# Scatters of a counting sort that wait one by one, four more blocks of it moved that way, and a reciprocal shared by two divisors

## The reference, cut to what matters

```python
# mixer of layer 0: linear attention on (1, 3125, ...) after a 5-tap convolution
q = relu(q); k = relu(k)
vk  = einsum('ngdl,ngel->ngde', v, k)
out = einsum('ngde,ngdl->ngdl', vk, q)
out = out / (sum(v, -1, keepdims=True) + 1e-15)     # with one position: v / (v + 1e-15), per element

# graph part of layer 0's feed-forward: 65536 random edges
e     = leaky_relu(a_src[src] + a_dst[dst])
alpha = exp(e - segment_max(e, dst)[dst]);  denom = segment_sum(alpha, dst)
agg   = segment_sum(h[src] * alpha / denom[dst], dst)
```

## Time and profile before

| | |
|---|---|
| time, median of 3 runs | 3484.07 us |
| profiled execution: span from first to last instruction | 3089.4 us |
| what lies around the span (median minus span) | 394.7 us |
| PE busy | 2176.1 us, 70% |
| DVE busy | 1707.6 us, 55% |
| POOL busy | 1668.6 us, 54% |
| ACT busy | 1346.5 us, 44% |
| mean granted PE clock | 0.844 |

### The profile page before, as it was taken

The page is one execution under the profiler, slowest core; times in us unless marked ns, Lnnn a source line. Parts: engine busy times, 40 slices in busy tenths (PEclk is TensorE's granted clock), DMA queues, the critical chain, the costliest instruction groups (busy, mean ns, idle before and its releaser), DMA issues. The chain is left out here.

```text
span 3089.4 us, 46006 instructions
## 1 busy us (share of the span) xinstructions
PE 2176.1 (70%) x14802; PEld 1673.9 (54%) x14802; DVE 1707.6 (55%) x3862; ACT 1346.5 (44%) x3168; POOL 1668.6 (54%) x1597
## 2 busy tenths in 40 slices
PE   4487292563399998376601586887786399999998
PEld 4362152453366665364301375666665266999997
DVE  7889545898311222989876666766665840111113
ACT  3368334774221221257903417677763021334432
POOL 0246564566277777877732555777772226344441
PEclk9799696787599999599955797888877589999999
DMA  3130034200223223245133345666662123356335
GB/s 91 62 123 1 18 67 78 49 1 1 42 49 83 43 43 76 48 117 118 10 94 60 62 122 187 214 212 203 201 206 89 51 80 92 120 195 222 122 123 130
DMA packets 183715, 301.48 MB, mean 98 GB/s; under 512 B 90826, under 2 KB 142653, under 8 KB 173096
## 3 DMA queue, kind: packets, MB, share of 16 engines
q1 hardware_dynamic: 104412, 168.04, 18.5%
q0 software_dynamic: 79168, 131.91, 16.1%
HBM read 266.22 MB, written 105.72 MB: 120 GB/s over the span
## 5 line engine op out<-in xcount | busy, mean ns | idle before, releaser
L1899 POOL DMA_INDIRECT ge_near<-gat_src,s_other x512 | 527.1, 1030 | 163.3 <-issue 157.2
L3253 POOL DMA_INDIRECT he_buf<-wh_dram,s_other x400 | 389.2, 973 | 160.4 <-issue 121.2
L982 POOL DMA_INDIRECT pl_table<-s_key,s_other x272 | 310.4, 1141 | 256.5 <-DMA pl_table<-s_key,s_other 181.9
L2764 ACT ACTIVATE x_hT<-bank,x_w 128x128 f32<-128x128 f32 x448 | 164.4, 367 | 262.6 <-PE bank L2707 231.4
L3373 ACT ACTIVATE he_buf<-he_buf,he_e 128x128 f32<-128x128 f32 x800 | 236.4, 386 | 2.8 <-issue 0.4
L2266 DVE TENSOR_TENSOR XN<-bank,arena 125x256 f32<-125x256 f32 (+1 forms) x100 | 42.5, 425 | 307.8 <-PE bank L2234 307.8
L2707 PEld LDWEIGHTS bank<-x_xT,x_w 128*128 128x128 f32 x1792 | 208.7, 192 | 2.8
L2707 PE MATMUL bank<-x_xT,x_w 128*128 128x128 f32 x1792 | 209.0, 275 | 0.0
L2717 PE MATMUL bank<-x_w,x_hT 128*128 128x256 f32 x896 | 202.5, 380 | 0.0
L3485 DVE SCALAR_TENSOR_TENSOR he_buf<-he_buf,he_cont 128x256 f32<-128x256 f32 x375 | 182.9, 488 | 29.2 <-issue 0.9
L2234 PE MATMUL bank<-arena 128*125 128x256 f32 x800 | 181.7, 385 | 23.2 <-ACT arena L2247 23.2
(11 more groups left out here) (749 smaller groups left out, 5694.1 us busy)
## 6 DMA issues: line engine op xcount, KB each, us to landing
he_result<-he_buf SPq DMA_DIRECT2D x25, 2080.0 KB, 7.8
XN<-s_a_dram SPq DMA_DIRECT2D x57, 512.0 KB
x_y<-XN SPq DMA_DIRECT2D x24, 448.0 KB
ge_near<-gat_src,s_other POOLq DMA_INDIRECT x512
x_x<-zero SPq DMA_DIRECT2D x1, 7196.0 KB, 44.2
x_xs<-x_x SPq DMA_DIRECT2D x56, 128.5 KB, 2.1
he_buf<-wh_dram,s_other POOLq DMA_INDIRECT x400
arena<-x_y SPq DMA_DIRECT2D x2, 2800.0 KB
```

The source lines that it names most:

```text
L982: pool.indirect_dma_start(out=self.table, out_offset=bass.IndirectOffsetOnAxis(ap=self.goal[:, c:c + 1], axis=0), in_=self.val[:, c:c + 1] ...
L1899: pool.indirect_dma_start(out=G[:, c, 0:HF + H], out_offset=None, in_=m.gat_src, in_offset=bass.IndirectOffsetOnAxis(ap=ed.other[:, c:c + ...
L2764: act.activation(self.hT[u % 2][:, f, :], m.ps[f % 4][:, 0:TS], ACT.Gelu, bias=self.rb1[u % self.B][:, f:f + 1]).then_inc(self.racted, 1)
L3253: pool.indirect_dma_start(out=buf[j][:, c, 0:HF + H], out_offset=None, in_=m.wh_dram, in_offset=bass.IndirectOffsetOnAxis(ap=ed.other[:, t ...
```

## The change

- `send`: three semaphores take turns. Scatter c waits, before it is issued, for scatter c-3 alone. The wait behind each third one is gone, also that behind the last of a stage.
- `BLOCKS` is 21 instead of 17: 336 scatters instead of 272, and 11 instead of 15 blocks in the product moves. They are dealt out as 64 in four batches with a `learn` each and 62 behind the fifth (126 in the sort), 34 at the start of `mix0_start` and 14 behind its gathers, 162 in `mix0_attention`.
- `load` waits for the three semaphores.
- `attend`: the 2048 divisors of a group (per partition) are cut into halves a and b. With va' = va + 1e-15 and vb' = vb + 1e-15 it forms va'·vb', takes one reciprocal of 1024 elements, and multiplies va by vb' and vb by va' before the shared reciprocal.

```diff
@@ mix0_start, gpsimd
-            placing.send(pool, 30)
+            placing.send(pool, 34)
             pool.wait_ge(nodes.w_ready, 1)
             pool.wait_ge(nodes.stored.sem, nodes.stored.all)
             edges.gather(pool)
+            placing.send(pool, 14)
@@ mix0_attention, gpsimd
-            placing.send(pool, 128)
+            placing.send(pool, placing.total - placing.begun)
@@ mix0_attention, attend
-                dve.tensor_scalar(o[:, 0:nt, :], vv[:, 0:nt, :], 1e-15, None, ALU.add)
+                va, vb, oa, ob = (x[:, 0:nt, h * HALF:(h + 1) * HALF] for x in (vv, o) for h in range(2))
+                dve.tensor_scalar(ob, vb, 1e-15, None, ALU.add)
                 dve.drain()
-                dve.reciprocal(o[:, 0:nt, :], o[:, 0:nt, :])
+                dve.scalar_tensor_tensor(oa, va, 1e-15, ob, ALU.add, ALU.mult)
+                dve.scalar_tensor_tensor(vb, va, 1e-15, vb, ALU.add, ALU.mult)
                 dve.drain()
-                dve.tensor_tensor(vv[:, 0:nt, :], vv[:, 0:nt, :], o[:, 0:nt, :], ALU.mult)
+                dve.reciprocal(oa, oa)
+                dve.tensor_tensor(va, va, ob, ALU.mult)
+                dve.drain()
+                both = vv[:, 0:nt, :].rearrange("p g (h c) -> p g h c", h=2)
+                dve.tensor_tensor(both, both, oa.unsqueeze(2).broadcast_to((P, nt, 2, HALF)), ALU.mult)
                 dve.drain()
@@ Placing
-    BLOCKS, TOGETHER = 17, 3
+    BLOCKS, FLYING = 21, 3
-        self.sent = m.sem("pl_sent")
+        self.sent = [m.sem(f"pl_sent{i}") for i in range(self.FLYING)]
@@ Placing.send
         for c in range(self.begun, self.begun + n):
+            landed = self.sent[c % self.FLYING]
+            if c >= self.FLYING:
+                pool.wait_ge(landed, 16 * (c // self.FLYING))
             pool.indirect_dma_start(out=self.table, ..., in_=self.val[:, c:c + 1], in_offset=None
-                                    ).then_inc(self.sent, 16)
-            if c % self.TOGETHER == self.TOGETHER - 1:
-                pool.wait_ge(self.sent, 16 * (c + 1))
+                                    ).then_inc(landed, 16)
@@ Placing.load
-        sp.wait_ge(self.sent, 16 * self.total)
+        for i, landed in enumerate(self.sent):
+            sp.wait_ge(landed, 16 * len(range(i, self.total, self.FLYING)))
@@ sort_edges, gpsimd
-                for t in range(3):
+                for t in range(4):
                     placing.learn(pool, s.pos, t + 1)
                     placing.send(pool, BC)
                 placing.learn(pool, s.pos, placing.BLOCKS)
-                placing.send(pool, 66)
+                placing.send(pool, 62)
```

More of the change, by code:

```diff
@@ L702, in mix0_attention @@
     O = GR * 32
+    HALF = O // 2
     z = [v.rearrange("p (g c) -> p g c", g=G) for v in (m.XN[:, 0:G * Z], m.sb("a0_z1", [P, G * Z])[:, :])]
@@ L981, in send @@
         for c in range(self.begun, self.begun + n):
+            landed = self.sent[c % self.FLYING]
+            if c >= self.FLYING:
+                pool.wait_ge(landed, 16 * (c // self.FLYING))
             pool.indirect_dma_start(out=self.table, out_offset=bass.IndirectOffsetOnAxis(ap=self.goal[:, c:c + 1], axis=0),
-                                    in_=self.val[:, c:c + 1], in_offset=None).then_inc(self.sent, 16)
-            if c % self.TOGETHER == self.TOGETHER - 1:
-                pool.wait_ge(self.sent, 16 * (c + 1))
+                                    in_=self.val[:, c:c + 1], in_offset=None).then_inc(landed, 16)
         self.begun += n
     def load(self, sp, back):
-        sp.wait_ge(self.sent, 16 * self.total)
+        for i, landed in enumerate(self.sent):
+            sp.wait_ge(landed, 16 * len(range(i, self.total, self.FLYING)))
         self.loaded(sp, back, self.rows())
```

## The result

The changed kernel took 3713.93 us, median of 4 runs (3691.22 to 3726.18), against 3482.05 us of the kernel before in the same measurement: a ratio of 1.067, interval 1.063 to 1.071. It is 232 us slower where 21 us less were forecast.

A forecast was written before the change was run, and what follows sets the result against it. POOL's scatters, with 181.9 us of landing waits, were taken to bound two of three barriers. Sort -32, mix0_start +1, attention +9 make -22 us, taken as 21: 3484 to 3463 us, range 3443 to 3484.

The forecast's parts named there:

- the base: Starting time: the 3484 us median stands for the profiled execution, span 3089.4 us and 394.7 us around it.
- None waits for ranks: 32 blocks are ranked until 234 us, 3.9 us each, so block 21 is known at about 191: Ranking in the sort: POOL's scatters never wait for ranks, so the first 64 end at 217.7 us.
- the terms for the product moves: Sort: four blocks fewer save 19.7 us; moves last till 301.5 us, with 36 scatters at 1.70 us.
- the attention's end: Attention on POOL: 561 + 184.8 + 45 + 1.5 = 792.3 us against 783.4; bounds 776 and 800.
- POOL was to be last at all three: Sign of being right: POOL arrives last at the barriers after the sort, mix0_start and the attention.
- a change behind 784 us: Stages after the attention: put at no change; a change of time there was named a sign of being wrong.
- Rival 2: All scatter stages: landings, not issues, set the pace; sort +23, mix0_start +21, attention +61 us, total 3589 us; chance 0.07.
- the mechanism of the forecast: Scatters in all three stages: without the old waits one takes 1.26 us undisturbed, its landing wait covered in quiet stretches.
- Sort: Sort stage: POOL free at 320 us instead of 352, 32 us gained; bounds 36.8 and 21 us gained.
- mix0_start: Second stage: POOL becomes last, 1 us lost; between 3 us gained and 4 us lost.
- Attention: Attention stage: DVE saves 19.7 us, covered by POOL; 9 us lost, between 7 us gained and 17 us lost.
- what the new half-size operations cost POOL: Attention: new two-input pair holds one scatter up by 1.7 us, the third adds 0.4; 7.4 us a group in all.

The follow-up runs named there:

- 3450 place: Measurement condition, not a kernel: the unchanged kernel before took 3482 us in one measurement of this kind and 3439 us in another.
- experiment 3: In one 3450 place, against the kernel before (1.003, unchanged): changed kernel 1.049; changed kernel with two scatters in flight 1.017, with one 1.104.
- 3090 place: Measurement condition, not a kernel: the unchanged kernel before took 3085 to 3094 us in four measurements of this kind.
- the rolling wait alone: Kernel before with each scatter waiting for the one three back, still 17 blocks and old reciprocal: 3064.34 us, ratio 0.990, in a 3090 place.

## Why the prediction was wrong, point by point

**The step that failed first: the base.** The prediction took 3089.4 us of span and "394.7 around it" as one execution. What lies around a span is 1.8 us in the changed kernel and 2.1 in the kernel before (3091.13 against 3089.0). So the 394.7 us were not around the span but inside the program, in executions that the profile did not show. In the 3450 place of experiment 3 the kernel before has 353.7 us more in its span, and in a stretch of it PE is idle beside close gathers as it is beside the scatters of the change; how much of the 353.7 us is of this kind was not added up. The gap stood in the table, and it was carried along as a constant.

**The step of the sum that failed: "None waits for ranks: 32 blocks are ranked until 234 us, 3.9 us each, so block 21 is known at about 191".** It takes PE, DVE and ACT to keep their pace however close POOL's scatters stand, and so do the terms for the product moves and for the attention's end. In the place that was measured, block 21 was known not at 191 but at 269.7, and POOL waited 61.66 us for it. At the barriers behind the sort and behind the attention DVE was last (idle for 1.31 and 1.18 us before its next work), where POOL was to be last at all three. In the 3450 place of experiment 3, where both kernels have a trace, the sort is 100.5 us longer than the kernel before's, mix0_start 30.7, the attention 46.1, the rest 8.6: together 185.9, the difference of the spans (168.4 by the medians). In the first measurement the same differences to that trace are 115.6, 31.0, 99.8 and 35.3; these are of two measurements. The prediction had no place for a change behind 784 us and had named one as a sign that it is wrong.

**Rival 2** (landings set the pace) had the sign, by the wrong mechanism: its waits did not come, 32.0 us of them in the whole program.

**In a 3090 place the mechanism of the forecast holds.** Its terms against the changed kernel's trace there:

```profile
314.96 0.96 POOL L993 DMA_INDIRECT pl_table<-s_key,s_other  x1 [0.30 <-issue]
...
322.33 4.02 DVE L474 BATCH_NORM_STATS2 l_stats<-X  x12 [7.31 <-PEq L73]
...
475.76 0.96 POOL L993 DMA_INDIRECT pl_table<-s_key,s_other  x1 [0.30 <-issue]
481.21 0.74 POOL L746 MEMSET a_pw<- 128x768 f32 x1 [4.49 <-POOLq L73]
...
575.39 1.23 DVE L888 SCALAR_TENSOR_TENSOR XT<-XT 125x1024 f32<-125x1024 f32 x1
575.84 1.62 POOL L993 DMA_INDIRECT pl_table<-s_key,s_other  x1 [0.30 <-issue]
577.83 6.55 DVE L891 RECIPROCAL XT<-XT 125x1024 f32<-125x1024 f32 x1
585.53 2.29 DVE L895 TENSOR_TENSOR XT<-XT 125x2048 f32<-125x2048 f32 x1
586.61 2.05 POOL L993 DMA_INDIRECT pl_table<-s_key,s_other  x1 [0.30 <-issue]
...
742.77 0.96 POOL L993 DMA_INDIRECT pl_table<-s_key,s_other  x1 [0.30 <-issue]
749.04 3.37 DVE L277 BATCH_NORM_STATS2 ln_stats<-X  x10 [25.12 <-PEq L73]
```

- Sort: DVE through at 315.0 (forecast 315.2), POOL at 315.9 (320), the barrier at 322.3 (327). 36 us gained, 32 forecast.
- mix0_start: POOL is last, at 476.7, as forecast; 4.0 us lost, 1 forecast, at its bound. The first 34 scatters take 49.5 us, some 52 forecast; the terms written out there are for 30 of them, which does no harm, since the gathers wait for the stores. They start 2.9 us earlier (3.3 forecast).
- Attention: DVE through at 723.9, 242.7 us into the stage against 262.3 of before: 19.6 us less (19.7 worked out), reciprocal 6.55 us. POOL is last. The stage is 3.2 us shorter, where 9 longer were forecast. The term that is off most is what the new half-size operations cost POOL: the scatter beside L888 and L889 takes 1.00 to 1.62 us, in the first group 1.72, at most 0.76 more than alone, where 1.7 more was put; beside the operations with 2048 elements it takes 2.05 to 2.07, once 1.93 and once 1.97 (before 2.07 and 2.88). The extra work is 28.5 us from the clearing on, some 4.7 us a group, which was the lower bound given, where 7.4 was put. The Trainium skill (SBUF — State Buffer, "Who interferes with whom") infers that a two-input operation of VectorE does not hold off descriptor generation; for 2048 elements the trace disagrees in this kernel too.
- The rest: 7.4 us more, in single executions. The sum of the four is 27.8 us gained by the spans; by the medians it is 34, against 21 forecast. That the sum lies within the forecast range is in part luck: the attention comes out 12 us better than forecast, and the rest, put at nothing, takes 7 back.

**Shown and not shown.** Shown: in a 3450 place PE is starved while POOL's scatters stand 1.26 us apart, in a 3090 place it is not, and in the 3450 place it nearly keeps its pace where they have breaks; the loss of the change in experiment 3 lies, but for 8.6 us, in the three stages in which its scatters stand close. Argued only: that the rolling wait alone carries the loss (with 17 blocks it makes the same unbroken row, but it was not timed in a 3450 place). Open: what differs between the places (the five measurements of the experiments are on five chips, one each, so chip and time are not told apart); why an instruction of PE comes every 1.4 us there; whether it takes a gap, a lower rate or an empty queue to feed it, and why the gathers of L401 do not starve it and those of L1518 do. The profile's two queues for instructions carry one and two packets from 119 to 335 us in the starved execution of experiment 3 (four and four from 119 to 322 us in the 3090 place), while PE got through fewer instructions; these counts show no crowding on the two queues, and they do not tell how long a fetch took.

## What to carry to other kernels

Hold the span of a profile against the listed time before anything else: some 2 us lay between them here when both were of one execution, and 394.7 when they were not. Where they differ like that, the profile is of other conditions, and the missing time belongs in the argument. A wait that looks wasted can be what lets other engines run: before closing the gaps in a row of DMAs issued by GpSimd, look for a stretch of the same program where they already stand close, and at what PE does beside it, in a trace that has the listed time. And time the parts alone and in pairs: the four more blocks brought nothing with the rolling wait, and hid what the reciprocal was worth (3043.8 us without them against 3059.6, both in one place).

## What the runs showed of the hardware that was not expected

- Beside indirect DMAs issued every 1.26 us, PE's instructions came 1.4 us apart in the 3450 places, with idle time marked "issue" (above, 312.72 to 316.92), 7 matmuls in 20 us in a window of experiment 3; beside 14 such scatters 362 in the 3090 place. Gathers every 1.52 us left PE its pace in both (141 and 140 matmuls in 75 us), others every 1.50 us did not (24 and 137 in 42 us). The Trainium skill (SBUF — State Buffer, "Who interferes with whom") says of PE and ACT that they never wait on anyone at the ports of SBUF; here both stand idle beside POOL's scatters all the same, and no run tells whether a port has a part in it. ACT's waits of 159.9 us carry the label "remote".
- With two scatters in flight, the one that waits for the second last starts 1.57 to 1.60 us behind the end of the last one in the rows of experiment 3, so some 2.9 us behind the end of the one that it waits for. These rows are of ranking, under large loads. With one in flight the wait there is mostly 2.5 to 3.1 us as well, and 1.42 to 1.44 us once the loads are over (timelines of that kernel; the mean of 1.66 us mixes the two):

```profile
166.68 0.96 POOL L993 DMA_INDIRECT pl_table<-s_key,s_other  x1 [2.93 <-DMA pl_table<-s_key,s_other]
...
388.16 0.96 POOL L993 DMA_INDIRECT pl_table<-s_key,s_other  x1 [1.43 <-DMA pl_table<-s_key,s_other]
```

So the 1.4 us of the prediction holds in quiet stretches, and a landing comes about twice as late under the loads, with or without another scatter behind it.
